# A masked and a cross attention block with a two-expert mixture on one core: another start-up, the second batch prepared three stages earlier, and the first and last self-attention prepared by halves

## The chip, the core and the metric

The kernel runs on one core of a Trainium2 chip. The core has five engines that run side by side, each with its own queue of instructions: TensorE (PE: matmuls and transposes), VectorE (DVE), ScalarE (ACT), GpSimd (POOL) and SyncE (SP, which here only starts DMAs). They meet through semaphores: an instruction that waits holds up everything behind it on its own engine. The metric is the time of one execution in microseconds (us), shorter being better.

## What is computed

Eight batches of 512 tokens of 256 numbers, 16 heads of 16. Per batch:

```python
x = x + tanh(g_xattn) * cross_attention(layernorm(x), ctx, ctx)      # no mask, no projections
n = layernorm(x)
h = n + self_attention(rmsnorm(n) * g1)       # q, k, v, o projections, rotary q and k, causal
y = h + mixture(rmsnorm(h) * g2)              # 8 experts, the best 2 of each token, 704 wide
out = x + tanh(g_ffn) * y
```

## The kernel before, in words

The program has two parts. The first (to about 1163 us) runs both attentions of all batches and scatters the routed tokens into `rows_in`; the second runs 71 tiles of 128 rows through the experts. The change touches the first part only.

**Units and stages.** An attention of one batch is four groups of four heads (g0 to g3). A group is done in two passes of 16 units. In a *max* unit PE multiplies a q tile with all k (L489, plus a mask matmul L492 for self-attention) and DVE takes the row maximum (`neg`, L811). In a *key* unit PE computes the transposed scores with the maximum folded in (L506, L509), ACT takes the exponential (`probs`, L680), and four value matmuls (L527) follow per key tile. Between the passes POOL splits the 16 maxima into three bfloat16 parts (`split_neg`, L1101 to L1104), PE turns them (`neg_turn`, L540), and ACT copies them and starts a DMA into the last rows of `q_stack` (L779, L781). q and k are used as three bfloat16 parts each (`parts_q`, `parts_k`), which are stored to DRAM (L384, six DMAs for each) and loaded back, six DMAs a group, as `q_stack[g]` and `k_stack[g]` (L377). There is one pair of these buffers for each group number.

**Steps.** `Step(i)` is a turn of eight stages s = 0..7, each of 16 places u. In step i the batch `cross` = i+1 is in cross attention, `own` = i in self-attention, `past` = i-1 finishes its self-attention and its output, and `ahead` = i+2 is prepared. Every engine walks the same steps, i from -2 to 8, and at fixed places u its `extra` function does the side work. `max_of(s)` and `main_of(s)` say which group has its max pass and which its key pass in a stage: stages 0 to 3 have the max passes of `cross`, 4 to 7 those of `own`; the key passes run two stages behind. A stage that has both passes is called double here, one with a single pass single. Below, c0 g2 is group 2 of the cross attention of batch 0, o7 that of the self-attention of batch 7.

**Side work.** For `ahead`: DVE statistics of x (stage 3), POOL normalises (`xq`), PE turns x and ctx (stages 4 and 5, `aux`), ACT copies to `flat_q`, `flat_k`, POOL splits into parts, SP stores them. For the next `own`, in stage 7: DVE adds the cross attention into x1 and takes statistics, POOL normalises (`xn`), and at the start of the next step ACT makes `hn1`. PE turns `hn1` at u = 4, 8; it projects q at 12, 13, 16, 17, k at 20, 21, 24, 25 and v at 31, 32, 37, 38, all through the one PSUM bank `aux`, which ACT empties after each half of 128 columns. DVE and POOL rotate q and k, POOL (in step 7 DVE for q) splits them. For `past`: output projection `wo` (u = 58 to 63), `h`, its root mean square (ACT squares, POOL `r_h`, L1082), router, and `scatter` (eight indirect DMAs on POOL, L1180). In every step -1 to 6 POOL also splits the weights of one expert in eight *pieces* (`split_piece`, L1074 to L1078), pieces 0 to 5 in stages 0 to 5, 6 and 7 in stage 6. A piece waits until the store of the piece before has landed, since both use the one buffer `w_parts`:

```python
step.wait(pool, m["w_in_ld"], (e * n + (k + 1)) * 16)
step.wait(pool, m["w_part_st"], (e * n + k) * 16)
```

Step -2 has no attention: it prepares batch 0 through `aux` alone. Step 7 (`LAST`) has the key passes o6 g2, g3 in stages 0, 1, no attention in 2 and 3, the max passes of o7 in 4 to 7 and key passes o7 g0, g1 in 6, 7; step 8 has o7 g2, g3.

## Time and profile before

| | us |
|---|---|
| three timed runs, median (lowest to highest) | 1715.73 (1715.44 to 1720.02) |
| profiled execution, its own time | 1707.33 |
| its span, first to last instruction | 1705.6 |
| PE, DVE, POOL, ACT busy, of the span | 1482.6, 976.2, 932.4, 807.1 |
| mean granted clock of PE | 0.946 of 2.4 GHz |

The profiled execution lies 8.4 us below the median of the timed runs. PE being busy for 87% of the span does not mean that it is at its peak all that time: in many stages its matmuls wait for their partners, and busy intervals include that pipelining. Places in the program are found by time: the first max matmul starts at 40.96, step 1 begins at 246.9, step 7 at 1010.6, the last exponential ends at 1114.4, the second part begins at about 1164.

### The profile page before, as it was taken

How to read it: one execution, taken by the hardware profiler on the slowest of the kernel's cores; microseconds unless marked ns; L12 is line 12 of the kernel's file. 1: busy time of each engine (PE TensorE's matmuls, PEld its weight loads, DVE VectorE, ACT ScalarE, POOL GpSimd, SP SyncE). 2: the span in 40 equal slices, each digit the busy share in tenths (PEclk: the TensorE clock that was granted, in tenths of full speed). 3: DMA queues.
4: the chain of work that ended last, by engine and by line, in shares of the span. 5: the costliest groups of instructions: out<-in, count | busy, mean ns of one | idle time of the engine just before them, and what ended most of it. 6: DMA issues, size and time to landing. Idle time of an engine off the chain costs nothing. (4 is left out here: it accounts for less than half of the span.)

```text
span 1705.6 us, 33019 instructions
## 1 busy us (share of the span) xinstructions
PE 1482.6 (87%) x9936; PEld 936.1 (55%) x9936; DVE 976.2 (57%) x2345; ACT 807.1 (47%) x1845; POOL 932.4 (55%) x1153
## 2 busy tenths in 40 slices
PE   1966989999999989989989987942999999999997
PEld 0212344444444444444443443432999999999997
DVE  1826667677677677677677555522444444444443
ACT  0451755755755755755755753521333333333332
POOL 5276766678678678678678353221334334433443
PEclk9987999989989999999999988966999999999999
DMA  5545564556455555556455434116142443244211
GB/s 171 156 128 157 162 180 134 155 158 199 151 171 186 155 173 183 160 173 186 147 182 163 145 121 111 63 37 255 54 147 60 151 150 122 93 151 151 61 57 32
DMA packets 112509, 238.41 MB, mean 140 GB/s; under 512 B 20624, under 2 KB 74772, under 8 KB 110295
## 3 DMA queue, kind: packets, MB, share of 16 engines
q1 hardware_dynamic: 76198, 147.66, 28.4%
q0 software_dynamic: 22656, 78.48, 13.4%
q10 hardware_dynamic: 13488, 10.17, 2.2%
q8 instruction: 91, 1.49, 0.4%
q14 instruction: 76, 0.61, 0.1%
HBM read 144.14 MB, written 93.14 MB: 139 GB/s over the span
## 5 line engine op out<-in xcount | busy, mean ns | idle before, releaser
L811 DVE TENSOR_REDUCE neg<-max_ps 128x1 f32<-128x512 f32 (+3 forms) x1024 | 564.6, 585 | 297.9 <-PE max_ps L492 150.1
L680 ACT ACTIVATE probs<-key_ps 128x512 f32<-128x512 f32 (+3 forms) x1024 | 499.5, 520 | 348.8 <-PE key_ps L509 197.8
L489 PE MATMUL max_ps<-k_stack,q_stack 96*128 96x512 bf16 (+3 forms) x1024 | 365.4, 362 | 75.0 <-DVE neg L811 33.9
L506 PE MATMUL key_ps<-q_stack,k_stack 99*128 99x512 bf16 (+3 forms) x1024 | 356.1, 351 | 22.7 <-ACT probs L680 17.5
L489 PEld LDWEIGHTS max_ps<-k_stack,q_stack 96*128 96x128 bf16 x1024 | 102.2, 100 | 293.3 <-DVE neg L811 173.4
L506 PEld LDWEIGHTS key_ps<-q_stack,k_stack 99*128 99x128 bf16 x1024 | 101.6, 100 | 153.4 <-ACT probs L680 92.7
L1448 PE MATMUL y_ps<-weights,hidden_t 128*128 x1278 | 171.4, 290 | 4.8 <-issue 3.4
L1448 PEld LDWEIGHTS y_ps<-weights,hidden_t 128*128 128x128 f32 x1278 | 158.3, 194 | 6.7 <-issue 6.7
L1424 PE MATMUL gate_ps<-weights,rows_t 128*128 x852 | 156.2, 332 | 6.5 <-DMA weights<-w_split 5.3
L1348 DVE TENSOR_TENSOR hidden<-silu,up_ps 128x352 f32<-128x352 f32 x142 | 74.0, 521 | 137.4 <-PE up_ps L1424 137.4
L1424 PE MATMUL up_ps<-weights,rows_t 128*128 x852 | 148.4, 323 | 0.0
L1295 POOL TENSOR_TENSOR more<-part,so_far 128x256 f32<-128x256 f32 x71 | 51.9, 731 | 175.3 <-issue 120.2
L527 PE MATMUL pv_ps<-probs,v_cross 128*32 128x512 f32 x1024 | 137.7, 605 | 4.5 <-ACT out_t L774 4.5
L1424 PEld LDWEIGHTS gate_ps<-weights,rows_t 128*128 128x128 f32 x852 | 137.1, 190 | 8.1 <-issue 7.9
L1424 PEld LDWEIGHTS up_ps<-weights,rows_t 128*128 128x128 f32 x852 | 139.0, 189 | 0.0
L1395 ACT ACTIVATE hidden_t<-hid_ps 128x512 fp32r<-128x512 f32 (+1 forms) x142 | 61.9, 488 | 151.7 <-PE hid_ps L1437 151.7
L1285 POOL DMA_INDIRECT so_far<-out,whose x71 | 73.0, 1028 | 101.8 <-issue 52.1
L1374 ACT ACTIVATE rows_t<-rows_ps,g_sb 128x128 fp32r<-128x128 f32 x142 | 44.4, 364 | 163.7 <-PE rows_ps L1409 163.7
L492 PE MATMUL max_ps<-squares_b 128*128 128x128 bf16 x512 | 117.7, 230 | 0.0
L509 PE MATMUL key_ps<-squares_b 128*128 128x128 bf16 x512 | 115.4, 226 | 0.0
L1299 POOL DMA_INDIRECT out<-more,whose x71 | 72.7, 1024 | 60.6 <-POOL more L1295 57.1
L527 PE MATMUL pv_ps<-probs,v_own 128*32 128x512 f32 (+3 forms) x1024 | 104.0, 477 | 1.7 <-ACT out_t L774 0.7
(182 smaller groups left out, 2115.8 us busy)
## 6 DMA issues: line engine op xcount, KB each, us to landing
w_split<-w_parts POOLq DMA_DIRECT2D x32, 704.0 KB
weights<-w_split SPq DMA_DIRECT2D x8, 2816.0 KB, 11.0
weights<-w_split SPq DMA_DIRECT2D x8, 1280.0 KB, 13.1
rows<-rows_in ACTq DMA_DIRECT2D x71, 129.0 KB
w_split<-w_parts POOLq DMA_DIRECT2D x16, 512.0 KB
kept_sb<-kept SPq DMA_DIRECT2D x16, 512.0 KB, 5.8
parts_cross_q<-parts_q SPq DMA_DIRECT2D x48, 128.0 KB
parts_cross_k<-parts_k SPq DMA_DIRECT2D x48, 128.0 KB
```

The source lines that it names most:

```text
L489: r = mm(ps[:, 0:keys], q_stack[g][0:KROWS, hd, qt * P:(qt + 1) * P], k_stack[g][0:KROWS, hd, 0:keys], start=True, stop=not own)
L492: r = mm(ps[:, qt * P:keys], ident_b, mask_qk, start=False, stop=True)
L506: r = mm(ps[:, q0:S], k_stack[g][0:KROWS + NEGROWS, hd, kt * P:(kt + 1) * P], q_stack[g][0:KROWS + NEGROWS, hd, q0:S], start=True, stop=no ...
L509: r = mm(ps[:, q0:q0 + P], ident_b, mask_kq, start=False, stop=True)
L527: mm(pv_ps[32 * hd:32 * hd + 32, q0:S], v_of["own" if own else "cross"][:, kt, g * HG + hd, :], probs[:, kt % 2, hd, q0:S], start=(kt == 0 ...
L680: act.activation(probs[:, kt % 2, hd, q0:S], key_ps[j % 2][:, q0:S], ACT.Exp).then_inc(m["exp_done"], 1)
L811: v.tensor_reduce(neg[:, g % 2, hd, qt:qt + 1], max_ps[(n * 16 + j) % MAX_RING][:, 0:keys], op=ALU.max, axis=AX.X, negate=True).then_inc(m ...
L1285: g_.indirect_dma_start(out=so_far[j % 2][:, :], out_offset=None, in_=out_rows, in_offset=bass.IndirectOffsetOnAxis(ap=whose[j % OWNERS][: ...
L1299: g_.indirect_dma_start(out=out_rows, out_offset=bass.IndirectOffsetOnAxis(ap=whose[j % OWNERS][:, 0:1], axis=0), in_=more[j % 2][:, :], i ...
L1348: v.tensor_tensor(hidden[:, n * FH:(n + 1) * FH], silu[:, n * FH:(n + 1) * FH], up_ps[n][:, 0:FH], ALU.mult)\
L1424: r = mm(ps[n][:, 0:FH], rows_t[:, a, c, :], weights[:, bass.ds(off + (w_ * WALL + at + c * F + n * FH), FH)], start=(c == 0 and (a, w_) = ...
L1448: r = mm(y_ps[:, 0:D], hidden_t[:, a, k, :], weights[:, bass.ds(off + (w_ * WALL + 2 * WG + k * D), D)], start=(k == 0 and (a, w_) == PASS ...
```

## The change

- **Start-up.** Step -2 is gone. Batch 0 is prepared by code of its own: the `k_stack` memsets go from POOL to DVE; SP loads the identity second and most constants late; PE turns ctx first and then x into four free banks; k half 0, q half 0 and q half 1 are split by DVE, k half 1 by POOL. SP then issues the loads of x and ctx of batch 1 (the latter waits for POOL's copy `v_cross`), stores half 0 of k and q, loads group 0, and stores half 1. Halves have their own semaphores.
- **Steps -1 and 0.** x and ctx of batch 1 are prepared in stages 0 to 2 of step -1 (statistics in stage 0, turned at u = 24, 28, 32, 36). The max passes of c1 are in stages 4 to 7 of step -1, its key passes in stages 0 to 3 of step 0. Step 0 has no max pass in stages 0 to 3 and no key pass in 4 and 5. Nothing changes in stages 6 and 7 of step 0.
- **Steps 0 and 7 (`alone`).** `hn1` is turned at u = 2, 4; the projections come as q0, k0, q1, k1, each whole at one place (6, 8, 10, 12), in step 0 v at 14 and 17. DVE rotates and splits each q half as it comes, POOL each k half in stage 0. SP stores q0, k0, loads group 0, then stores q1, k1.
- **Pieces.** Expert e is now split in step e, not e-1: none in step -1; in step 7 two in each of the stages 4 to 7. In step 7 both scatters of batch 5 come after the k split, in stage 1.
- The seven stores of `padding` move from the start to step 0. In steps 1 to 6 each engine does the same work in the same order.

```diff
     def max_of(self, s):
-        u = self.named("cross" if s < 4 else "own")
+        if self.i == -1 and s >= 4:
+            return ("cross", 1, 1, s - 4)
+        u = None if self.i == 0 and s < 4 else self.named("cross" if s < 4 else "own")
         return u and (*u, s % 4)
 
     def main_of(self, s):
-        which, g = [("past", 2), ("past", 3), ("cross", 0), ("cross", 1), ("cross", 2), ("cross", 3), ("own", 0), ("own", 1)][s]
-        u = self.named(which)
+        order = FIRST_MAINS if self.i == 0 else MAINS
+        which, g = order[s]
+        u = which and self.named(which)
         return u and (*u, g)
 
     def tail_of(self, s):
-        return self.main_of(s - 1) if s else self._past(1)
+        return self.main_of(s - 1) if s else Step(self.i - 1).main_of(7)
 
     def neg_of(self, s):
-        return self.max_of(s - 1) if s else self._past(3)
-
-    def _past(self, g):
-        u = self.named("past")
-        return u and (*u, g)
+        return self.max_of(s - 1) if s else Step(self.i - 1).max_of(7)
+
+
+MAINS = [("past", 2), ("past", 3), ("cross", 0), ("cross", 1), ("cross", 2), ("cross", 3), ("own", 0), ("own", 1)]
+FIRST_MAINS = [("cross", 0), ("cross", 1), ("cross", 2), ("cross", 3), (None, 0), (None, 0), ("own", 0), ("own", 1)]
...
 PIECES_AT = ((0,), (1,), (2,), (3,), (4,), (5,), (6, 7), ())
-
-
-def splits_on_dve(step):
-
-    return step.i in (-2, LAST)
+LAST_PIECES_AT = ((), (), (), (), (0, 1), (2, 3), (4, 5), (6, 7))
+
+
+def alone(step):
+
+    return step.i in (0, LAST)
+
+
+def turned_at(step):
+
+    return (24, 28, 32, 36) if step.i == -1 else (72, 76, 80, 84)
+
+
+def parts_made(step, b, c, n, of_own):
+
+    if of_own and alone(step) or not of_own and b == 0:
+        return b * 6 + 3 * c + n + 1
+    return b * 6 + 2 * (n + 1)
...
+def qk_order(step):
+
+    return [("q", 0), ("k", 0), ("q", 1), ("k", 1)] if alone(step) else [("q", 0), ("q", 1), ("k", 0), ("k", 1)]
...
+                    if step.i == 0:
+                        for n in range(SPARE):
+                            sp.dma_start(rows_in[E * CAP + n * P:E * CAP + (n + 1) * P, :], padding[:, :]).then_inc(m["ld_pad"], 16)
...
-                sp.wait_ge(m["ready_v"], 1)
-                for n in range(SPARE):
-                    sp.dma_start(rows_in[E * CAP + n * P:E * CAP + (n + 1) * P, :], padding[:, :]).then_inc(m["ld_w"], 16)
-                def sp_body(step):
-                    if step.i == -2:
-
-                        store_parts(step, "cross", "q", 0, "x_parts", "x_st")
-                        store_parts(step, "cross", "k", 0, "c_parts", "c_st")
-                        load_stack(step, "cross", 0, 0, 0)
...
+                sp.dma_start(rope_sb[:, :, :], c_rope).then_inc(m["ld_const"], 16)
+                sp.dma_start(g1_sb[:, :], g1.rearrange("(c p) -> p c", p=P), allow_slow_non_contiguous=True).then_inc(m["ld_const"], 16)
+                sp.dma_start(g2_sb[:, :], g2.rearrange("(c p) -> p c", p=P), allow_slow_non_contiguous=True).then_inc(m["ld_const"], 16)
+                load_x(Step(-1))
+                first = Step(-2)
+                store_half(first, "k", "c", 0, 0)
+                store_half(first, "q", "x", 0, 0)
+                load_stack(first, "cross", 0, 0, 0)
+                store_half(first, "k", "c", 0, 1)
+                store_half(first, "q", "x", 0, 1)
+
+                run_steps(sp, body)
...
-                        for c, at in enumerate((4, 8)):
+                        for c, at in enumerate((2, 4) if alone(step) else (4, 8)):
                             if u == at:
                                 step.wait(pe, m["x1_norm"], own + 1)
                                 turn("hn1", own, c, hn1)
-                        for k, at in enumerate((12, 13, 16, 17)):
+                        halves = qk_order(step)
+                        for k, at in enumerate((6, 6, 8, 8, 10, 10, 12, 12) if alone(step) else (12, 13, 16, 17, 20, 21, 24, 25)):
...
+                    if own is not None and alone(step):
+                        for c, where_ in enumerate(((0, 2, 0), (0, 3, 2))):
+                            if at == where_:
+                                own_half(step, c)
...
...
+                dve.wait_ge(m["x_ld"], 16)
+                for t in range(QT):
+                    r = v.bn_stats(st_x[:, t, :], x_in[:, t, :])
+                chain.link(r)
+                for t in range(QT):
+                    r = v.bn_aggr(mv_x[:, t, :], st_x[:, t, :])
+                r.then_inc(m["x_stat"], 1)
+                aux_free(dve, "c", 0, 0)
+                split(flat_k, parts["k"], 0, "c_parts", 0)
+                for c in range(DC):
+                    aux_free(dve, "x", 0, c)
+                    split(flat_q, parts["q"], c, "x_parts", 3 * c)
...
                     for s in range(8):
-                        if s == 0 and step.cross is not None:
-                            load_piece(step.cross, 0)
-                        if s == 0 and done is not None:
+                        if s == 0 and step.own is not None:
+                            load_piece(step.own, 0)
+                        if s == 0 and done is not None and step.i != LAST:
                             scatter(done, 0)
                         extra(step, s)
-                        if s == 1:
+                        if s == 1 and not alone(step):
                             rotate(step, 1)
+                        if s == 2 and step.i == -1:
+                            split_ahead(step, "k")
                         ng = step.neg_of(s + 1) if s < 7 else Step(step.i + 1).neg_of(0)
-                        pieces_ = PIECES_AT[s] if step.cross is not None else ()
+                        pieces_ = (LAST_PIECES_AT if step.i == LAST else PIECES_AT)[s] if step.own is not None else ()
                         for k in pieces_[:-1]:
                             split_piece(step, k)
                         if ng and s:
                             split_neg(step, ng)
-                        if s == 1:
+                        if s == 1 and step.i == -1:
+                            split_ahead(step, "q")
+                        if s == 1 and not alone(step) or s == 0 and alone(step):
                             rotate(step, 2)
+                        if s == 1 and done is not None and step.i == LAST:
+                            scatter(done, 0)
+                            scatter(done, 1)
                         for k in pieces_[-1:]:
                             split_piece(step, k)
-                        if s == 0 and done is not None:
+                        if s == 0 and done is not None and step.i != LAST:
                             scatter(done, 1)
                         if ng and not s:
                             split_neg(step, ng)
 
...
+                split(None, flat_k, parts["k"], "c_parts", 0, 1)
+                g_.tensor_scalar(v_of["cross"][:, :, :, 0:DH].rearrange("p t h d -> p (t h) d"),
+                                 ctx_in[:, :, :].rearrange("p t (h d) -> p (t h) d", d=DH), 1.0, 0.0, ALU.mult, ALU.add)\
+                    .then_inc(m["v_cross"], 1)
```

SP at the start of the program; `parts_cross_k` and `parts_cross_q` are the stores of batch 0, `q_stack` and `k_stack` the loads of its groups. Before:

```order
L439 DMA rows_in<-padding 128x258 x7
L384 DMA parts_cross_q<-parts_q 8x16x512 x6
L384 DMA parts_cross_k<-parts_k 8x16x512 x6
L377 DMA q_stack<-parts_cross_q 48x1x2048
L377 DMA q_stack<-parts_cross_q 32x1x2048
```

After:

```order
L383 DMA x_in<-in_x 128x4x256
L387 DMA ctx_in<-in_ctx 128x4x256
L412 DMA parts_cross_k<-parts_k 8x16x512 x3
L412 DMA parts_cross_q<-parts_q 8x16x512 x3
L407 DMA q_stack<-parts_cross_q 48x1x2048
```

Group 0 is loaded after six stores in place of twelve, and the input loads of batch 1 now stand ahead of the first store.

PE in stage 0 of step 7, from the turn of the first half of `hn1` (the key matmuls of o6 g2 between). Before, to the first projections of q:

```order
L559 MATMUL aux<-ident,hn 128x128 x4
L506 MATMUL key_ps<-q_stack,k_stack 128x256
L509 MATMUL key_ps<-squares_b 128x128
L506 MATMUL key_ps<-q_stack,k_stack 128x256
L509 MATMUL key_ps<-squares_b 128x128
L527 MATMUL pv_ps<-probs,v_own 32x384 x4
L506 MATMUL key_ps<-q_stack,k_stack 128x256
L509 MATMUL key_ps<-squares_b 128x128
L506 MATMUL key_ps<-q_stack,k_stack 128x256
L509 MATMUL key_ps<-squares_b 128x128
L552 MATMUL turn_ps<-ident,out_t 128x128 x4
L566 MATMUL aux<-hn_t,sb_wq 128x512
```

After, from the first projection of q to that of the second half:

```order
L620 MATMUL aux<-hn_t,sb_wq 128x512 x2
L560 MATMUL key_ps<-q_stack,k_stack 128x384
L563 MATMUL key_ps<-squares_b 128x128
L560 MATMUL key_ps<-q_stack,k_stack 128x384
L563 MATMUL key_ps<-squares_b 128x128
L594 MATMUL turn_ps<-squares_b,neg_parts 48x128
L620 MATMUL aux<-hn_t,sb_wk 128x512 x2
L560 MATMUL key_ps<-q_stack,k_stack 128x256
L563 MATMUL key_ps<-squares_b 128x128
L560 MATMUL key_ps<-q_stack,k_stack 128x256
L563 MATMUL key_ps<-squares_b 128x128
L581 MATMUL pv_ps<-probs,v_own 32x384 x4
```

A projected half now stands every two key units, where before one stood every four.

POOL in step 7, from the root mean square of `h` (batch 6) on; `neg_parts` is the split of the maxima of o7 g0, then g1. Before:

```order
L1081 TENSOR_SCALAR tmp_r<-ss 128x4
L1082 TENSOR_TENSOR r_h<-tmp_r,half 128x4
L1101 TENSOR_SCALAR neg_parts<-neg 128x16
L1102 TENSOR_TENSOR neg_rest<-neg,neg_parts 128x16
L1103 TENSOR_SCALAR neg_parts<-neg_rest 128x16
L1104 TENSOR_TENSOR neg_parts<-neg_rest,neg_parts 128x16
```

After, from the end of g0's split to the start of g1's:

```order
L1207 TENSOR_TENSOR neg_parts<-neg_rest,neg_parts 128x16
L1177 TENSOR_SCALAR w_parts<-w_in 128x704
L1178 TENSOR_TENSOR w_parts<-w_in,w_parts 128x704
L1166 DMA w_in<-in_L_ffn_wu 128x704
L1181 DMA w_split<-w_parts 256x1x704
L1177 TENSOR_SCALAR w_parts<-w_in 128x704
L1178 TENSOR_TENSOR w_parts<-w_in,w_parts 128x704
L1166 DMA w_in<-in_L_ffn_wu 128x704
L1181 DMA w_split<-w_parts 256x1x704
L1204 TENSOR_SCALAR neg_parts<-neg 128x16
```

Piece 0 stands before g0's split, pieces 1 and 2 between g0 and g1, 3 and 4 between g1 and g2, 5 and 6 between g2 and g3.

## Rows read from the trace of the kernel before

**Rows 1.** Timeline of the start: start us, us, engine line op out<-in xcount [idle before]
```profile
10.95 1.33 DVE L875 BATCH_NORM_STATS2 st_x<-x_in 128x6 f32<-128x256 f32 x4
...
14.63 2.17 POOL L1091 TENSOR_SCALAR xq<-x_in,less_mean,r_x 128x256 f32<-128x256 f32 x4
...
25.83 6.42 SPq L384 DMA_DIRECT2D parts_cross_k<-parts_k  x6
...
28.91 2.12 POOL L1056 TENSOR_TENSOR parts_k<-rest,parts_k 128x1024 bf16<-128x1024 f32 x1
31.12 1.05 POOL L1157 TENSOR_SCALAR v_cross<-ctx_in 128x1024 f32<-128x1024 f32 x1
...
34.54 1.91 SPq L377 DMA_DIRECT2D q_stack<-parts_cross_q  x3
...
40.96 13.93 PE L489 MATMUL max_ps<-k_stack,q_stack 96*128 96x512 bf16 x24 [17.26 <-DMA k_stack<-parts_cross_k]
```
**Rows 2.** Groups by line, DVE: names, shapes, count | busy, mean ns | idle before
```profile
L1338 DVE MEMSET weights<- 64x1024 f32 x1 | 0.9, 912 | 8.8 <-PEq L238 8.8
```
**Rows 3.** Timeline between c0 and c1, the same columns
```profile
126.72 2.00 PE L489 MATMUL max_ps<-k_stack,q_stack 96*128 96x512 bf16 x4 [12.70 <-DMA k_stack<-parts_cross_k]
...
140.59 1.12 PE L559 MATMUL aux<-ident,hn 128*128 128x128 f32 x4 [11.86 <-ACT hn L700]
```
**Rows 4.** Busy time in stretches: stretch length, PE PEld DVE ACT POOL, clock, DMA
```profile
40.96:51.20 10.24, 10.16 (x18) 1.81 (x18) 9.62 (x17) 0.00 (x0) 0.00 (x0) 1.00 1.01 297
...
74.20:87.90 13.70, 13.11 (x74) 3.95 (x76) 12.07 (x27) 9.84 (x21) 7.25 (x14) 1.00 0.24 81
...
99.80:111.60 11.80, 10.75 (x62) 2.99 (x61) 0.68 (x2) 10.03 (x19) 11.06 (x9) 1.00 0.40 134
...
1010.60:1022.40 11.80, 10.03 (x78) 4.65 (x71) 1.25 (x4) 9.04 (x24) 7.15 (x12) 1.00 0.41 148
1022.40:1036.20 13.80, 13.76 (x87) 6.14 (x86) 11.10 (x20) 8.49 (x21) 1.92 (x2) 1.00 0.25 78
1056.90:1063.90 7.00, 6.36 (x35) 2.81 (x32) 6.85 (x17) 0.00 (x0) 0.00 (x0) 0.61 1.01 193
...
1105.40:1114.40 9.00, 8.02 (x72) 3.04 (x70) 0.68 (x2) 6.71 (x17) 3.86 (x4) 1.00 0.17 61
```
**Rows 5.** Timeline of step 7: a projected half, the end of `wo`, the first max matmul
```profile
1018.89 1.10 PE L566 MATMUL aux<-hn_t,sb_wq 128*128 128x512 f32 x2
...
1021.35 0.59 ACT L686 ACTIVATE flat_q<-aux 128x512 f32<-128x512 f32 x1
...
1046.86 1.99 PE L575 MATMUL aux<-sb_wo,own_t 128*128 128x256 f32 x8 [0.88 <-DVE h L891]
...
1056.52 0.29 PE L489 MATMUL max_ps<-k_stack,q_stack 96*128 96x128 bf16 x1 [7.67 <-DMA k_stack<-parts_own_k]
```
**Rows 6.** Timeline of POOL: pieces, their stores and the waits before them
```profile
123.86 0.40 POOL L1074 TENSOR_SCALAR w_parts<-w_in 128x256 fp32r<-128x256 f32 x1 [2.98 <-DMA w_split<-w_parts]
...
182.96 0.74 POOL L1078 DMA_DIRECT2D w_split<-w_parts  x1
...
189.25 0.78 POOL L1074 TENSOR_SCALAR w_parts<-w_in 128x704 fp32r<-128x704 f32 x1 [4.41 <-DMA w_split<-w_parts]
...
192.69 0.72 POOL L1078 DMA_DIRECT2D w_split<-w_parts  x1
...
198.38 0.78 POOL L1074 TENSOR_SCALAR w_parts<-w_in 128x704 fp32r<-128x704 f32 x1
```
**Rows 7.** Timeline of POOL in steps 7 and 8
```profile
1052.18 1.04 POOL L1082 TENSOR_TENSOR r_h<-tmp_r,half 128x4 f32<-128x4 f32 x1
...
1130.05 0.20 POOL L1081 TENSOR_SCALAR tmp_r<-ss 128x4 f32<-128x4 f32 x1 [19.67 <-ACT sq L733]
```
**Rows 8.** Timeline of ACT in step 8: the DMA of g3's maxima, the last exponential
```profile
1101.07 0.73 ACTq L781 DMA_DIRECT2D q_stack<-neg_rows  x1
...
1113.90 0.45 ACT L680 ACTIVATE probs<-key_ps 128x128 f32<-128x128 f32 x2 [0.51 <-PE key_ps L509]
```

346 lines of the change are left out of this document (213 added, 133 removed).

## The prediction, as written before the changed kernel ran

> **What bounds the kernel now.** I read the page for what is busy, the timeline for the three stretches that the change touches, the busy time by stage for prices, and the waits of POOL. In the middle of the program the stages are full: a double stage takes 13.7 us with PE busy for 13.1 [rows 4], and steps 1 to 6 are not changed. The time that could be won lies at both ends. At the start PE first has a max matmul at 40.96, held by the stack loads [rows 1]. Between the first and the second cross attention PE waits 12.7 us for loads and then 11.9 us for `hn1` [rows 3]. In step 7 PE has finished `wo` at 1048.85 and waits 7.67 us for the stacks of o7 [rows 5]. POOL is nowhere the bound as a whole, but it is one queue, and the maxima of each group pass through it.
>
> All times below stand against the profiled execution (span 1705.6); I carry the difference over to the median.
>
> **Start-up: 9.0 us less.** The four memsets cost DVE 2048 elements each; at the 912 ns for 1024 elements of [rows 2] that is 1.82 us each, 7.3 in all, from 0.75 to 8.05, and the small ones to 8.4. The statistics then begin 2.55 us before the 10.95 of [rows 1], and `xq` ends at 14.3 in place of 16.8. POOL splits k half 1 (half of 1.05 + 2.12 twice, with gaps 3.5) and copies `v_cross` (1.05): 19.0. Only then may SP issue ctx of batch 1 (0.55), and only behind it the stores: six at 0.61 (last three rows of six stores each take that) end at 23.3. From the last store's issue (32.25) to the first load's (34.54) is 2.3 us, and from there to the first matmul 6.4 [rows 1]: 25.6 and 32.0. DVE has q half 0 ready at 18.5, so it hides. 40.96 - 32.0 = 9.0. A bfloat16 memset on DVE isn't in the trace: at half the time all of this would come 3.6 us sooner, at half as much again 3.6 later; I take the float row, as the nearest.
>
> The Trainium skill ("VectorE: DVE Perf Modes", Zero memsets can be issued as uint32) says that a memset takes one cycle per element whatever the type, which agrees with taking the float row and speaks against the quicker case. The Trainium skill ("SBUF — State Buffer", Who interferes with whom) also says that a DVE instruction with two SBUF inputs and a GpSimd instruction that reads SBUF exclude each other; no row of before shows the two side by side in the start. By that rule DVE's two subtracts of a half (some 0.6 us each) could push `v_cross`, and the gain would be about 8 in place of 9.
>
> **From the first max pass to step 1: 4.0 us more.** Before it is 246.9 - 41.0 = 205.9, with both waits of [rows 3] in it. Prices: a single cross max stage 9.65 (10.2 to the next, DVE-bound), a double stage 13.7, a single cross key stage 11.8 with two turns of `aux`, so 11.5 without [rows 4]. After, step -1: stage 0 is 9.65 + 2.1 for the statistics that move into it = 11.8; stage 1 10.1 with two turns; stages 2 to 5 double, 13.8 + 13.5 + 13.6 + 13.6; stage 6 9.65 + 0.7 for the last cross group; stage 7 9.65 + 5.0 for x1's sums and statistics on DVE, which nothing hides now = 14.7. Together 101.5. POOL has no pieces there, so `xn` is ready when the stage ends. The stack loads of c1 are ready by my count some 3 us before each is due: the k split ends at about 68, the stores land at 72, g0 is loaded by 78 and due at 81.
>
> Step 0, stage 0, is the price of packing. A whole projected half is two calls of 1.10 on PE [rows 5]; behind it on PE stands the next key matmul (0.35), on ACT its exponential (0.6) and then the copy out of `aux` (0.59) before the next half may start: 4.0 us each, and only two key units go by. So: `hn1` 2.0 from the stage's start, two turns with copies 5.0, four halves 16.0, v, its copy and the last units 4.4: 27.4. In stage 1 the rest of v: 13.8. Stages 2, 3: 11.5 each. Stages 4, 5, single max passes of o0: 7.0 each as [rows 4] shows for o7, 7.2 + 7.8 with turns. But POOL must in these 15 us split q (6.7), g0's maxima, piece 4 (3.6), k (6.7) and g1's maxima: 4.2 us late in stage 5, 0.5 in stage 6. Stages 6 and 7 as before, 12.4 + 12.1. Together 108.4. 101.5 + 108.4 = 209.9, against 205.9. The idle 24.6 us go, but what was a double stage becomes single ones (six doubles in place of eight), and stage 0 grows. Bounds: if the halves fit between key units as they do before, 8 us less, that is 4 us better than before; if POOL is later by one piece's landing, 5 more.
>
> **Step 7 up to the max passes of o7: 1.1 us less, not 7.7.** Before, stages 0 and 1 took 11.8 + 13.8 = 25.6, all projections and half of v in them; stage 1 of step 8, with a group and nothing beside it, is 9.0 [rows 4]. After, stage 0 by the same handover (4.0, less 0.2 for shorter exponentials): 2.0 + 4.5 + 15.2 + 1.2 = 22.9, stage 1 9.3: 32.2, 6.6 more. `wo` ends at 1048.85 + 6.6 = 1055.4. The stacks have long landed then: the k parts of half 0 are ready at about 1032.5, and 2.3 + 6.4 later is 1041.8. So the DMA wait of 7.67 goes, and PE's own order takes its place; 1055.4 against 1056.5.
>
> **The pieces in step 7: 16.8 us more.** (Times here are in before's clock; the parts above shift them all.) `r_h` ends at 1053.2 [rows 7]; it follows `h`, which follows `wo`, so it comes 6.6 later, 1059.8. Everything behind it on POOL is one chain: a piece, then the landing of its store, since the next piece waits for that. A 704-wide piece takes 193.41 - 189.25 = 4.16. From the end of a store's issue to the next piece are 189.25 - 183.70 = 5.55, and another piece did not have to wait after 4.97 [rows 6]. I take 5.0 for pieces 0 to 3, since little else moves in step 7. For a 512-wide store POOL copied `v_cross` (1.1) and then waited 2.98 [rows 6]: 4.1. Pieces of 512 and 256 take 3.6 and 2.8, scaled from the same rows. Up to g3's split: four pieces 16.6, four landings 20.0 (the base of `out`, 3.6, lies in the last), then 3.6, 4.1, 3.6, 4.1, 2.8 and the split 1.1: 55.9. So g3's maxima are split at 1115.7. From there it is 1.0 to ACT's DMA, and from that to the end of the exponentials 1114.35 - 1101.07 = 13.3 [rows 8]: 1130.0. Before it is 1114.35: 15.7 later, and as this holds the 1.1 won above, the pieces cost 16.8. PE waits for each split at its place, so the stalls show at the turns of g1 (some 6), g2 (5) and g3 (4); behind a turn on PE are the second half of the stage's units, and ACT and DVE wait for those. After piece 7 POOL scatters batch 6 (13 us), done at about 1133; what it owes next is `r_h` of batch 7, which started at 1130.05 [rows 7] and now would near 1146: hidden. The second part starts later by the same 15.7.
>
> **Sum.** -9.0 + 4.0 - 1.1 + 16.8 = +10.7 us: a span of 1716.3, and 1715.7 + 10.7 = 1726.4 for the timed median.
>
> **Rivals.** (1) *The middle wins more than I count.* The halves of step 0 fit between key units and POOL keeps up in stages 4 and 5: -9.0 - 4.0 + 15.7 = +2.7, 1718.4. For it: 24.6 us of idle time do go [rows 3]. Against: `aux` is one bank, and four handovers stand in eight places. (2) *The pieces in step 7 are covered*, the one that ends faster. Six landings stand in the chain, 28.2 us. If they averaged 2.9 instead of 4.7 the whole change would come to zero, and from 1.9 down no turn waits: -9.0 + 4.0 - 1.1 = -6.1, 1709.6. For it: step 7 moves little else. Against: the shortest landing in the rows is 4.1. A better start and middle with half the stalls gives about the same time. (3) *More stalls.* Landings 0.6 longer each, as in [rows 6], make 3.6; and the clock granted after PE's idle 7.67 us was 0.61 [rows 4], which behind three stalls may add 4: 1734. (4) *The start doesn't come sooner*, since the first store still stands behind POOL's copy: with that at 25 in place of 19, 6 of the 9 us are lost: 1732.
>
> **How the numbers follow.** Changes under 0.3% (5 us) can't be told from none here. Forecast, 3 to 17 us slower: 0.55, of which 0.03 under 5 us. Rival 1: 0.19, within. Rival 2 and what leads to its time: 0.16. Rival 3: 0.06, rival 4: 0.04. Slower: 0.52 + 0.10 = 0.62; within 0.22; faster 0.16. The range leaves out rival 2's lower half and what lies beyond rival 3: 1710 to 1734.
>
> **What would show it.** First max matmul at 32; start of step 1 at 242; the first max matmul of o7 right behind `wo` with no DMA wait, in absolute time 6 us earlier (9 - 4 + 1); gaps of PE before the turns of g1, g2 and g3 in steps 7 and 8, ended by POOL's splits, with POOL waiting for `w_split`; last exponential at about 1125. I am wrong if those turns don't wait, or if stage 0 of steps 0 and 7 takes under 20 us.

## The result and the profile after

The changed kernel takes 1733.55 us (median of six, 1729.14 to 1738.29), the kernel before 1718.44 (1715.44 to 1721.94): a ratio of 1.0087, 95% interval 1.0064 to 1.0110, or 11 to 19 us slower. Forecast was 10.7 slower and 1726.4, in a range of 1710 to 1734: the result lies 0.5 us inside its upper end, and the kernel before itself came out at 1718.44 here, where the forecast had been added to 1715.73.

The span can be cut at six events that every trace shows: the first max matmul, the first reduction of c2 (start of step 1), the first exponential of o6 g2 (start of step 7), the first reduction of o7, the last exponential, the end. Each entry below is the difference of two start or end times of such rows. Both kernels were profiled twice.

```
kernel           to first   to      steps   step 7 up  passes  to the  span
                 max mm     step 1  1 to 6  to o7      of o7   end
before             41.0     206.0   763.6     46.4      57.4    591.2   1705.6
before, again      41.0     205.7   766.1     46.0      58.7    590.1   1707.6
changed            36.4     210.2   769.6     45.3      77.3    592.7   1731.4
changed, again     36.4     210.1   765.9     45.5      74.6    591.7   1724.3
forecast change    -9.0      +4.0     0       -1.1     +16.8     0       +10.7
measured (means)   -4.6      +4.3    +2.9     -0.8     +17.9    +1.6     +21.3
```

The profiles differ by 21 us where the timed medians differ by 15. Both profiles of before lie below its median (1707.3 and 1709.4 of a median of 1714 to 1720 in the later comparisons), so single profiles are good for the place of a change, not for its last microseconds.

The start after (timeline: start us, us, engine, line, operation, out<-in, count), which answers to [rows 1]:

```profile
18.58 0.98 DVE L910 TENSOR_TENSOR turned<-flat_q,parts_q 128x512 f32<-128x512 f32 x1
...
19.59 1.26 DVE L911 CAST parts_q<-turned 128x512 bf16<-128x512 f32 x1
...
20.66 1.10 POOL L1346 TENSOR_SCALAR v_cross<-ctx_in 128x1024 f32<-128x1024 f32 x1
20.89 1.40 DVE L913 TENSOR_TENSOR parts_q<-turned,parts_q 128x512 bf16<-128x512 f32 x1
21.84 0.37 SPq L387 DMA_DIRECT2D ctx_in<-in_ctx  x1
22.25 2.02 SPq L412 DMA_DIRECT2D parts_cross_k<-parts_k  x3
...
24.32 1.81 SPq L412 DMA_DIRECT2D parts_cross_q<-parts_q  x3
...
29.81 1.90 SPq L407 DMA_DIRECT2D q_stack<-parts_cross_q  x3
...
36.37 1.98 PE L543 MATMUL max_ps<-k_stack,q_stack 96*128 96x512 bf16 x4 [17.62 <-DMA k_stack<-parts_cross_k]
```

Two things are to be seen: the first store is issued right behind POOL's copy and the ctx load, at 22.25, and DVE's split of q half 0 ends only at 22.29.

POOL in step 7 after (timeline), which answers to [rows 6] and [rows 7]: `r_h`, the pieces, g3's split.

```profile
1066.16 1.05 POOL L1185 TENSOR_TENSOR r_h<-tmp_r,half 128x4 f32<-128x4 f32 x1
1067.21 0.77 POOL L1177 TENSOR_SCALAR w_parts<-w_in 128x704 fp32r<-128x704 f32 x1
...
1083.86 0.78 POOL L1177 TENSOR_SCALAR w_parts<-w_in 128x704 fp32r<-128x704 f32 x1 [4.22 <-DMA w_split<-w_parts]
...
1097.57 2.34 POOL L1271 TENSOR_TENSOR base_sb<-base_sb,kept_sb 128x1024 f32<-128x1024 f32 x1
...
1117.39 0.40 POOL L1177 TENSOR_SCALAR w_parts<-w_in 128x256 fp32r<-128x256 f32 x1 [4.27 <-DMA w_split<-w_parts]
...
1121.10 0.22 POOL L1207 TENSOR_TENSOR neg_parts<-neg_rest,neg_parts 128x16 bf16<-128x16 f32 x1
```

And the stages there (busy time in stretches: length, then PE PEld DVE ACT POOL, granted clock, DMA share, GB/s), from stage 0 of step 7 to the last exponential; before, the first three are 11.8, 13.8 and 20.7 long [rows 4, 5]:

```profile
1016.10:1036.90 20.80, 17.25 (x92) 7.58 (x85) 10.08 (x19) 10.76 (x27) 4.71 (x8) 0.92 0.26 89
1036.90:1046.70 9.80, 8.88 (x72) 3.94 (x71) 7.25 (x11) 6.83 (x17) 6.86 (x7) 1.00 0.28 73
1046.70:1061.40 14.70, 10.41 (x53) 7.48 (x51) 1.93 (x4) 2.88 (x5) 8.15 (x11) 0.88 0.82 223
1061.40:1069.70 8.30, 5.65 (x30) 1.76 (x30) 6.84 (x18) 3.75 (x12) 7.14 (x8) 0.88 0.58 170
1069.70:1078.80 9.10, 8.03 (x41) 4.82 (x41) 6.36 (x17) 1.68 (x4) 5.27 (x10) 0.55 0.34 122
1078.80:1097.60 18.80, 17.21 (x119) 9.24 (x119) 11.09 (x37) 7.33 (x19) 10.65 (x16) 0.64 0.41 138
1097.60:1115.20 17.60, 12.96 (x100) 6.46 (x101) 12.31 (x30) 7.30 (x18) 9.79 (x13) 0.81 0.59 206
```

The key stages of o7 g0 and g1 take 18.8 and 17.6 where they took 12.6 and 12.3 before, and 13.4 and 13.7 in its second profile (first exponential of a group to that of the next). PE looks busy in the first of them, at a granted clock of 0.64, near the lower of its two levels (1.2 of 2.4 GHz); the matmuls stretch to fill the time that POOL's chain leaves.

The largest waits of PE in the passes of o7 (timeline): the turns of the maxima of g0, g1 and g3 wait for POOL, the third unit of g3's max pass for DVE. The turn of g2, at 1109.20, does not wait.

```profile
1072.65 0.30 PE L594 MATMUL turn_ps<-squares_b,neg_parts 128*48 128x128 bf16 x1 [0.89 <-POOL neg_parts L1207]
...
1089.20 0.30 PE L594 MATMUL turn_ps<-squares_b,neg_parts 128*48 128x128 bf16 x1 [1.46 <-POOL neg_parts L1207]
...
1103.10 0.29 PE L543 MATMUL max_ps<-k_stack,q_stack 96*128 96x128 bf16 x1 [3.87 <-DVE neg L883]
...
1121.38 0.24 PE L594 MATMUL turn_ps<-squares_b,neg_parts 128*48 128x128 bf16 x1 [1.67 <-POOL neg_parts L1207]
```

### The profile page after: what moved, and what is told of

It is laid out like the page before. It is cut to its first block and busy times, and to the rows that moved or that the text cites. A ratio compares the mean times of both kernels' runs of the same rounds, so it can differ in the third digit from the quotient of the medians.

```text
span 1731.4 us, 33153 instructions
## 1 busy us (share of the span) xinstructions
PE 1505.1 (87%) x9936; PEld 943.1 (54%) x9936; DVE 1007.8 (58%) x2375; ACT 806.3 (47%) x1845; POOL 914.4 (53%) x1155
## 3 DMA queue, kind: packets, MB, share of 16 engines
q0 software_dynamic: 22656, 78.48, 13.3%
## 5 line engine op out<-in xcount | busy, mean ns | idle before, releaser
L1535 ACT ACTIVATE hidden_t<-hid_ps 128x512 fp32r<-128x512 f32 (+1 forms) x142 | 61.9, 488 | 151.6 <-PE hid_ps L1577 133.8
L1425 POOL DMA_INDIRECT so_far<-out,whose x71 | 73.0, 1028 | 101.5 <-issue 44.3
```

Of the source, the lines that this page charges most:

```text
L1425: g_.indirect_dma_start(out=so_far[j % 2][:, :], out_offset=None, in_=out_rows, in_offset=bass.IndirectOffsetOnAxis(ap=whose[j % OWNERS][: ...
```

## The experiments

Both kernels were profiled once more, and ten further kernels ran; each was timed beside the kernel before on the same chip. One table for the ten, in the cuts of the first, from one profile each; the ratio is that of timed runs to the kernel before.

```
run            first  to      steps   to o7  passes  end    ratio (95%)
               mm     step 1  1 to 6         of o7
pieces_early   37.9   216.8   769.5   45.3   57.9   591.1   1.0047 (1.0026 to 1.0068)
ctx_later      31.3   211.0   766.0   45.3   73.0   589.9   1.0039 (1.0015 to 1.0063)
mid_before     39.6   212.7   765.9   45.4   62.1   591.0   0.9997 (0.9979 to 1.0014)
spread         36.4   210.7   773.6   44.7   77.0   596.2   1.0086 (1.0061 to 1.0111)
two_parts      36.0   206.3   770.8   47.3   67.2   590.4   1.0004 (0.9986 to 1.0022)
before_swap    40.8   206.6   768.6   47.5   60.2   587.7   0.9980 (0.9956 to 1.0004)
last_early     36.4   207.3   768.7   45.5   73.7   592.0   1.0063 (1.0034 to 1.0093)
all_three      31.3   205.6   765.6   47.3   67.8   595.9   1.0000 (0.9968 to 1.0033)
all_swap       31.4   203.2   759.0   45.3   69.8   592.8   0.9959 (0.9935 to 0.9983)
final          31.2   203.3   759.2   45.3   62.9   593.8   0.9905 (0.9869 to 0.9941)
```

### Both kernels again

Each was profiled once more, unchanged.

> The kernel before, unchanged, profiled a second time. In its first profile steps 1 to 6 (from the first max group of c2 to the second exponential group of step 7's stage 0) take 763.6 us, and in the profile of the changed kernel 769.6, though their work and order are the same. If that is a price of the change, this run shows 763 to 765 again and a span near 1706. If it is only the spread of one execution (the timed runs of before reach 1721.9, 14 above its profile), this run shows a middle of 766 to 770 and a span of 1711 to 1718.

> The changed kernel, unchanged, profiled a second time. First max reduction at 37, step 1 at 246 to 247, steps 1 to 6 in 765 to 770, last exponential of own attention 7 some 122 to 123 after step 7's start (before: 103.8). If the half clock at 1070 to 1100 belongs to the order of step 7 it is there again; if it came by chance it is gone, and the last exponential comes 5 or more sooner.

Steps 1 to 6 of before came at 766.1, those of the changed kernel at 765.9. So the 6 us of the first pair were mostly spread, yet not all (below). The passes of o7 took 74.6, at a clock of 0.75, so the low clock belongs to the order of step 7. The turns of g0, g1 and g3 waited 2.4, 2.5 and 1.5, that of g2 not at all, as in the first profile.

### The pieces one step sooner (pieces_early)

```diff
-LAST_PIECES_AT = ((), (), (), (), (0, 1), (2, 3), (4, 5), (6, 7))
+FIRST_PIECES_AT = ((), (), (0,), (1,), (2,), (3,), (4, 5), (6, 7))
...
-                    e = step.own
+                    e = step.cross
...
```

> As the changed kernel, but each weight piece is split one step sooner: step -1 takes expert 0's (stages 2 to 7), and step 7 has none. My theory (the pieces of step 7 cost 16.8 by my count, 19.9 by the traces): the max and key passes of o7 take 50 to 58 us from the first reduction to the last exponential in place of 77, and the whole is 15 to 20 us shorter than the changed kernel: 1714 to 1719, some 0.2% below before to equal; step -1 grows by 0 to 4 us. Rival (the time went to the low clock that PE's idle stages in step 7 bring, not to the pieces): the granted clock in the max passes of o7 stays at 0.6, the passes still take 65 us or more, and the whole is 1725 or more.

The o7 passes, first reduction to last exponential (busy time in a stretch):

```profile
1069.50:1127.40 57.90, 51.64 (x429) 25.18 (x430) 33.77 (x102) 32.67 (x86) 19.09 (x33) 0.94 0.21 69
```

57.9, as before the change: the 18 us there are the pieces. The clock is 0.94 over the stretch, so the rival falls. But the total won only 7 us against the changed kernel's ratio of 1.0087. In steps -1 and 0 the pieces cost 6.7 and at the start 1.5: c1's first group waited 3.3 us for its `k_stack`, `hn1` came 2.7 us later. I had put 0 to 4 on that. There was nothing to spare for it: in the changed kernel itself c1's first stacks landed at 83.5 and PE waited 0.5 us for them, where the prediction had counted on 3 us in hand.

### The context load behind the first stacks (ctx_later)

```diff
-                load_x(Step(-1))
                 first = Step(-2)
+                first.wait(sp, m["x_norm"], 1)
+                sp.dma_start(x_in[:, :, :], x_d[1]).then_inc(m["x_ld"], 16)
...
                 store_half(first, "q", "x", 0, 1)
+                aux_full(sp, "c", 0, DC - 1)
+                first.wait(sp, m["v_cross"], 1)
+                sp.dma_start(ctx_in[:, :, :], ctx_d[1]).then_inc(m["ctx_ld"], 16)
```

> As the changed kernel, but the load of batch 1's context, which waits for POOL's copy of v_cross, is issued behind the first eighteen stores and loads instead of ahead of them. My theory (the first store waits for that copy, which ended at 21.8): the first store is issued at about 19.5 when the first half of q is split, the first max matmul comes at 33.5 to 34.5 instead of 36.4, and the whole is 2 to 3 us shorter. Rival (POOL's own split of k's second half ends late too, or the loads' landing sets the time): under 1 us.

```profile
16.65 2.02 SPq L412 DMA_DIRECT2D parts_cross_k<-parts_k  x3
...
18.71 4.18 SPq L412 DMA_DIRECT2D parts_cross_q<-parts_q  x3
...
24.94 1.90 SPq L407 DMA_DIRECT2D q_stack<-parts_cross_q  x3
...
31.34 1.98 PE L547 MATMUL max_ps<-k_stack,q_stack 96*128 96x512 bf16 x4 [12.60 <-DMA k_stack<-parts_cross_k]
```

The first max matmul came 5.0 us sooner, twice what I expected. The stores ended 3.2 us sooner, at 22.9, now waiting for q's last part (DVE, 22.3) and not for POOL's copy; and the time from the last store to the first load was 2.1 in place of 3.7. What else is in that 1.6 was not taken apart; the load of ctx, issued just ahead of the stores in the changed kernel, no longer runs beside them. Of these 5 us 0.8 is lost on the way to step 1 (211.0 against 210.2). The ratio fell by more than 2 to 3 us (from 1.0087 to 1.0039, some 8 us), of which the start explains 5.

### The start and step 7 alone (mid_before)

Taken back: max passes of c1 in step 0, batch 1 prepared in stages 4 to 6 of step -1, step 0 as before, pieces a step sooner.

```diff
-        if self.i == -1 and s >= 4:
-            return ("cross", 1, 1, s - 4)
-        u = None if self.i == 0 and s < 4 else self.named("cross" if s < 4 else "own")
+        u = self.named("cross" if s < 4 else "own")
...
-    return (24, 28, 32, 36) if step.i == -1 else (72, 76, 80, 84)
+    return (72, 76, 80, 84)
```

> Only the new start-up and the halves of step 7: batch 1 is prepared in step -1's stages 4 to 6 and c1's max passes stand in step 0's stages 0 to 3, as before, step 0 projects as before, and the pieces stand where they did before. My theory (the parts add up): first max matmul at 36.4 to 37.9, from it to step 1 205.9 as before, step 7 up to the max passes of o7 45.4 (before 46.2), the passes of o7 58: 4 to 5 us shorter than before. Rival (the idle in step 0 ends with a load that comes no sooner, so the early start is given back there): step 1 still starts at 246 to 247, the interval from the first matmul grows to 209 or more, and the whole is 0 to 1.5 us shorter than before.

The rival holds in what it says of the gain, though step 1 began later than it said, at 252.2. The start itself is worth only 1.4 us when the first weight piece is loaded, split and stored beside it (the first stacks landed 3.2 us later than in the changed kernel). The two waits of [rows 3] came back, 12.4 and 12.1 us, and from the first matmul to step 1 it took 212.7 in place of 206. Of that, 5.5 us are one wait:

```profile
PE max_ps L529 <- DMA k_stack<-parts_cross_k: 5.5, 1, 5.5
```

It stands at 251.6: the seven stores of `padding`, which the change put into step 0, are issued from 227.0 to 230.4 ahead of the stores of c2's parts, and group 0 of c2 landed at 251.5, in the second profile of before at 246.2. In the changed kernel step 0's stacks are ready sooner and the same stores delay nobody. Without that wait step 1 would begin near 246.7 (an estimate: 252.2 less 5.5), where it begins in before: with the old middle the sooner start is given back, and the stores of `padding` in step 0 make it worse. The passes of o7, with no piece in them, took 62.1 and not the 58 expected; with the 57.4 to 60.2 of the other profiles without pieces there, that is how far this stretch moves when nothing of the pieces is in it.

### Halves further apart (spread)

```diff
-                        for k, at in enumerate((6, 6, 8, 8, 10, 10, 12, 12) if alone(step) else (12, 13, 16, 17, 20, 21, 24, 25)):
+                        for k, at in enumerate((6, 7, 10, 11, 14, 15, 18, 19) if alone(step) else (12, 13, 16, 17, 20, 21, 24, 25)):
...
-                        for t, at in enumerate((14, 14, 17, 17) if step.i == 0 else (31, 32, 37, 38)):
+                        for t, at in enumerate((22, 23, 26, 27) if step.i == 0 else (31, 32, 37, 38)):
...
```

> As the changed kernel, but in steps 0 and 7 the halves of q and k are projected at every fourth unit (6, 10, 14, 18) instead of every second (6, 8, 10, 12), v of step 0 at 22 and 26. My theory (each half waits for the copy of the half before it, behind a key unit: 4 us for a half whose neighbours are two units off): stage 0 of step 0, 26.0 now, and stage 1, 13.3, together lose 6 to 8; stages 0 and 1 of step 7, 20.6 + 9.8, lose 3.5 to 5, if the stacks of o7 still land before wo ends; the whole 8 to 12 us shorter than the changed kernel. Rival (PE's work and the arrival of hn1 set those stages, not the handovers): both change by under 2 us, or the stacks become the last and o7's first max matmul waits for a load as before.

My theory fell. Stages 0 and 1 of step 0 took 21.8 + 16.1 in place of 25.8 + 13.3, 1.2 less in all, and what was won there was gone by the end of step 0; up to o7 step 7 won 0.7. The packing moves time between two stages, it does not cost 4 us a half. It also tells of the pieces: the o7 passes took the same 77.0 us, but with PE busy for 55.2 of them in place of 61.5 and at a clock of 0.84 in place of 0.78. With the faster matmuls the waits show: the turns of g0, g1 and g3 waited 4.6, 4.8 and 1.5, in place of 0.9, 1.5 and 1.7. Not PE and not its clock set this stretch.

### Two buffers for the pieces (two_parts)

```diff
-s1("w_parts", 2, F, dt=F32R)
+s1("w_parts", 2, 2, F, dt=F32R)
...
-                    step.wait(pool, m["w_part_st"], (e * n + k) * 16)
+                    half_ = k % 2
+                    step.wait(pool, m[f"w_part_st{half_}"], (e * n // 2 + k // 2) * 16)
...
```

> As the changed kernel, but two buffers take the split weight pieces in turn, so that a piece waits for the store of the piece before the last. My theory (in step 7 POOL's chain of pieces and landings sets the turns of g1 to g3; seven landings of 4 us lie in it): the maxima of g3 are split some 12 to 20 us sooner, no turn of step 7 waits, and from the first reduction of o7 to the last exponential it takes 58 to 65 in place of 75 to 77; whole 12 to 18 shorter than the changed kernel. Rival (the half clock of the stretch, which lies in order and idle of PE, sets it): 70 or more, and under 5 us on the whole.

```profile
1060.30:1127.50 67.20, 55.01 (x430) 26.11 (x430) 37.80 (x102) 33.13 (x86) 44.46 (x63) 0.89 0.43 146
```

67.2: half way, between the 58 to 65 expected and the 70 of the rival. Without most of the landings 8.8 of the 17.9 us go. The rest goes with POOL's own work there (44.5 us busy in 67, 15.0 of 57.4 in before) and what it does to DVE, shown below; how it divides was not measured. A second gain I had not expected lies in step 0, 3.9 us: the interval to step 1 fell to 206.3, since stage 4 of step 0 takes 9.2 when POOL's pieces there don't wait, in place of 12.7:

```profile
195.10:204.30 9.20, 7.87 (x57) 4.21 (x56) 7.19 (x18) 3.11 (x6) 4.29 (x5) 1.00 0.86 268
```

### The maxima ahead of the second scatter (before_swap)

```diff
+                        if ng and not s:
+                            split_neg(step, ng)
                         if s == 0 and done is not None:
                             scatter(done, 1)
-                        if ng and not s:
-                            split_neg(step, ng)
```

> The kernel before with one exchange: in stage 0 of each step POOL splits the maxima of c's first group ahead of the second scatter of the past batch, not behind it. Reason: in the profiles stage 1 of steps 2 to 6 takes 17.7 in some steps and 18.5 to 23 in others; where it is long, POOL stood for the landing of the first scatter, its split of the maxima ended 7 to 8 us after the reductions, PE's turn waited 1.4 to 1.6 for it, and the granted clock then fell to 0.6. My theory: that turn no longer waits in any step, stage 1 takes 17.5 to 17.9 in all of them, steps 2 to 6 take 630 or less (631 and 634 before; 637 to 641 in the changed kernel), and the whole is 1 to 5 us shorter than before and its spread smaller. Rival (the clock falls there for PE's own sparse stage, and q's rotation comes later instead): no change, or up to 3 us longer.

Inconclusive in time (0.9980, up to 1.0004). Stage 1 took 17.8 in four of the five steps 2 to 6 and 21.5 in one, where the turn did not wait at all. So my reason was wrong. Nor did steps 2 to 6 get shorter: they took 638.3, against 631.2 and 634.2 in before and 630 or less expected, since stage 0 took 15.7 to 16.0 in each step where it took 15.0 in both profiles of before. Then I looked at what DVE did in the long stages 1. In the second profile of the changed kernel, step 4:

```profile
657.02 2.13 POOL L1156 TENSOR_TENSOR rest<-flat_q,parts_q 128x1024 f32<-128x1024 f32 x1
...
657.12 2.58 DVE L917 TENSOR_TENSOR with_cos<-flat_k,rope_sb 128x512 f32<-128x512 f32 x1
...
660.97 0.39 PE L543 MATMUL max_ps<-k_stack,q_stack 96*128 96x512 bf16 x1 [2.26 <-DVE neg L883]
```

and at the same place of step 4 in the later run all_swap:

```profile
641.77 0.72 DVE L921 TENSOR_TENSOR with_cos<-flat_k,rope_sb 128x512 f32<-128x512 f32 x1
642.04 2.44 POOL L1160 TENSOR_TENSOR rest<-flat_q,parts_q 128x1024 f32<-128x1024 f32 x1
...
643.79 0.39 PE L547 MATMUL max_ps<-k_stack,q_stack 96*128 96x512 bf16 x1 [0.42 <-DVE neg L887]
```

DVE's multiply of two SBUF operands takes 0.7 us when it comes first, and 2.58 when POOL's subtract started 0.1 us ahead of it: 0.55 us and the 2.03 that POOL still had to go. So it is in the fourteen traces, five such stages each, wherever the subtract had a lead of 0.1 us or more: the multiply takes 0.55 us and what POOL still has to go. Once the lead was 0.015 us, and it was the subtract that took longer (2.68). In 26 of the 70 the multiply took under 1 us, and stage 1 took 18.0 on the mean; in 33 it took 1.5 us or more, and the stage took 19.9 (18.6 to 23.1). The two go together; no run changed the multiply alone. In three of the 33, one each in both profiles of before and in before_swap (the 21.5), the subtract had not begun, and the 1.57 us began beside the cast that POOL makes ahead of it. In the long stage shown above PE idles 2.3 us for DVE, and in the 4.6 us that follow the granted clock is 0.63:

```profile
657.00:661.00 4.00, 1.74 (x20) 0.91 (x19) 4.00 (x6) 1.01 (x4) 3.67 (x3) 1.00 0.22 66
661.00:665.60 4.60, 4.60 (x16) 3.06 (x17) 4.23 (x10) 0.55 (x2) 2.08 (x2) 0.63 0.10 29
```

The Trainium skill ("SBUF — State Buffer", Who interferes with whom) says that a DVE instruction with two SBUF inputs contends with a GpSimd instruction that reads SBUF, the later one being blocked as a whole; these rows agree, in both directions, but for some 0.14 us: the multiply was 1.9 longer, where POOL had 2.03 to go, and the subtract 0.31 longer, where DVE had 0.45 to go.

### Five pieces ahead of o7 (last_early)

```diff
-LAST_PIECES_AT = ((), (), (), (), (0, 1), (2, 3), (4, 5), (6, 7))
+LAST_PIECES_AT = ((0, 1, 2), (3, 4), (), (), (), (5,), (6,), (7,))
...
+                        if step.i == LAST and s < 2:
+                            for k in pieces_:
+                                split_piece(step, k)
+                                if s == 1:
+                                    scatter(done, k - 3)
...
```

> As the changed kernel, but five of step 7's eight weight pieces are split before the max passes of o7: 0 to 2 in stage 0 ahead of k's halves, 3 and 4 in stage 1 beside the scatters; 5, 6 and 7 follow the maxima in stages 5 to 7. Nothing is left out, one buffer as before. My theory (what costs is the place: eight pieces and their landings between the r_h of batch 6 and g3's maxima): three pieces are left there, the passes of o7 take 58 to 62 in place of 75 to 77, and the whole is 13 to 18 us shorter than the changed kernel. Rival (POOL's time in step 7 is short everywhere): k's second half is split later, so the stacks of o7 land behind wo, the first max matmul of o7 waits 3 us or more, and half of the gain is lost.

73.7: nearer to the rival. Its cause came true in part. Behind pieces 0 to 2 the split of k's second half ended 3.4 us ahead of o7's first max matmul, where it ended 10.3 ahead in the changed kernel; g0's stacks were still in time, but g1's `k_stack` came 5.5 us late. Pieces 3 and 4 beside the scatters kept POOL from g0's maxima, whose turn waited 5.4 us. No later turn waited: the waits moved from the turns of g1 and g3 to the beginning, and nearly the whole gain was lost.

### Combinations (all_three, all_swap, final)

all_three is ctx_later, two_parts and last_early together; all_swap adds the exchange of before_swap.

> The changed kernel with three edits together: the context load of batch 1 behind the first stacks, two buffers for the split pieces, and five pieces of step 7 ahead of o7. If the prices of the single runs add up: first max matmul at 31.3, from it to step 1 206 to 207, step 7 up to the passes 45 to 47, the passes of o7 57 to 61: step 1 starts at 238, and the whole is 8 to 14 us shorter than before (ratio 0.992 to 0.995). Rival (they share one gain, the buffers mattering only where the pieces stand late, or steps 2 to 6 give it back, which took 637 to 641 in four profiles with the new middle and 631 and 634 in two of before): ratio 0.997 or more.

> The same with the exchange that was made alone in before_swap: in stage 0 POOL splits the maxima of c's first group ahead of the second scatter. In before_swap stage 1 took 17.8 in four of the five steps 2 to 6, and here it takes 18.5 to 20 without the exchange. My theory: stage 1 takes 17.8 in most steps and steps 2 to 6 take 632 to 635 in place of 637 to 641, so the whole is 3 to 6 us shorter than the run without the exchange. Rival: one step in five loses 4 us all the same to the low clock, and no difference shows.

all_three matched before (1.0000): start and middle came as added up (31.3 and 205.6), but two pieces and the scatters stood ahead of g0's maxima again, and the passes of o7 took 67.8, not 57 to 61. With the exchange the multiply came ahead of POOL's subtract in all five steps, stage 1 took 18.0 in each, and steps 1 to 6 took 759.0 in place of 765.6. It helps not by the wait I had named; that POOL's time in stage 1 then no longer hangs on the landing of a scatter is my reading of the order, which no run separates. The two instructions pass each other by 0.3 us, so this is a matter of luck in another kernel.

final has pieces 0 and 1 ahead of k's halves, one behind each of g0, g1, g2, and three behind g3:

```diff
-LAST_PIECES_AT = ((), (), (), (), (0, 1), (2, 3), (4, 5), (6, 7))
+LAST_PIECES_AT = ((0, 1), (), (), (), (2,), (3,), (4,), (5, 6, 7))
...
```

> The changed kernel with the context load behind the first stacks, two buffers for the split pieces, the exchange of stage 0, and the pieces of step 7 put where POOL stood idle: 0 and 1 in stage 0 ahead of k's halves, 2, 3 and 4 each behind the maxima of g0, g1 and g2, 5 to 7 behind those of g3; none between k's second half and g0's maxima. My theory (the turns of g1 to g3 waited for pieces ahead of the maxima, and in the two runs before this for two pieces ahead of g0's): no turn of step 7 waits 1 us or more, no load holds o7's max passes, these take 57 to 60 (before 57.4 to 60.2, the changed kernel 75 to 77), from the first matmul to step 1 203 to 206, steps 2 to 6 631 to 633: a span near 1690, a ratio of 0.987 to 0.991. Rival (the pieces behind g3's maxima push the scatter of batch 6 and the r_h of batch 7, so that the routing and the second part begin later): from the last exponential to the end 597 or more in place of 590 to 593, and a ratio of 0.993 or more.

```profile
1039.10:1102.00 62.90, 56.56 (x429) 26.90 (x430) 35.64 (x102) 32.88 (x86) 35.01 (x53) 0.84 0.39 126
```

1697.94 us, median of six, a ratio of 0.9905 (0.9869 to 0.9941) to the kernel before: it beats both kernels. No turn of o7's maxima waits more than 0.2 us, and the passes take 62.9; 57 to 60 was expected. PE is busy for 56.6 of them, where the same matmuls took 52.1 of the 57.4 before, at a clock of 0.92. The stretch to the end is 593.8, 2.6 and 3.7 more than in the two profiles of before, and short of the 597 of the rival.

## Why the prediction was right, and where not

That the change costs time, and that the pieces in step 7 make it so, was right and is shown. The total came near by errors of both signs; term by term:

**Start: -9.0 forecast, -4.6 measured.** The mechanism was right, the sizes of three terms were not. The statistics began at 9.78, not at 8.4: the memsets took 1.76 each (the float row was the right neighbour), but with 0.38 between them and from 1.23 on. POOL's split of k half 1 took 4.4 and not 3.5. And "DVE has q half 0 ready at 18.5" failed: it was ready at 22.3, 1.9 for the later `xq` and 1.8 because DVE and POOL split side by side and held each other up (1.26 for a cast that took 0.43 with the next half, 1.40 and 0.98 for subtracts that took 0.69). The rule was weighed at 1 us in all; it took 1.8 from DVE and 0.6 from POOL's split. Here POOL's copy ended at about the same time and hid it; in ctx_later it was what the stores waited for. The last 1.4 us are the 3.7 from the last store to the first load, for which I had taken before's 2.3. Rival 4 named the right instruction, POOL's copy ahead of the first store; it came at 21.8, half way between 19 and 25.

**First max pass to step 1: +4.0 forecast, +4.3 measured, by luck: its errors cancel.** Step -1 took 97.1 and not 101.5, for x1's sums and statistics fit into its last stage (11.9, forecast 14.7). Step 0 took 113.1 and not 108.4. Its stage 0 was near (25.8, forecast 27.4), though the reason given for it, the handovers, was refuted by spread. Stages 4 to 7 took 51.2 in place of 44.2: I priced a single max pass of o0 with the 7.0 of o7 [rows 4], and it takes 9.2 there even without a wait, and POOL, late by its pieces' landings, held `xq` for 2.0, a turn for 5.3 and another for 1.8. two_parts took 3.9 of this away.

**Steps 1 to 6: 0 forecast, +2.9 on the mean of two.** "Are not changed" holds for the order, not for the phase. Step 1 is 3.7 shorter on the mean (128.3 and 128.4 against 132.4 and 131.8), nearly all in its stage 0, where PE's wait for exponentials, 3.2 us at 251.6 in before, is 1.7; spread and last_early, whose step 1 is that of the changed kernel, took 131.5 and 133.8, so this is no firm gain. Steps 2 to 6 take 641.2 and 637.5 against 631.2 and 634.2, in two places. Stage 1 took 95.9 and 96.9 in the five steps, against 91.3 and 92.2, with DVE's multiply at 1.5 us or more in six of ten stages against three of ten. And stage 0 took 82.0 in the first profile of the changed kernel, against 75.2 in its second and in both of before. In nine of the fourteen profiles stage 0 takes 15.0 in each of these steps and in five 15.6 to 16.0 (one stage 18.8), and both lengths occur with and without the change. What sets either phase is open.

**Step 7 up to o7: -1.1 forecast, -1.1 and -0.6 measured.** PE's own order took the place of the wait for a load, as said; stages 0 and 1 took 30.6 (forecast 32.2).

**Pieces in step 7: +16.8 forecast, +17.9 measured (19.9 and 15.9 in the two pairs), and pieces_early shows that it is they.** The chain on POOL from `r_h` to g3's split took 54.1 (forecast 55.9), with 4.0, 4.2, 4.0, 3.6, 5.9 and 4.3 between the end of a store's issue and the next piece. The size is right for a chain with two errors in it: `r_h` came 2.2 later against the first matmul of o7 than forecast, behind the second scatter of batch 5, and from g3's split to the last exponential it took 17.4, not 14.3, at a clock of 0.90. The stalls did not show where they were forecast: at the turns of g1, g2 and g3 (6, 5, 4) they are 1.5, 0 and 1.7, in the second profile 2.5, 0 and 1.5, and that of g0, for which none was forecast, waits 0.9 and 2.4. The rest shows as matmuls stretched by the low clock and as one wait of 3.9 us (3.0 in the second profile) for DVE at g3's third unit. So the chain on POOL was right, and where PE would stand for it was not. DVE was held there by POOL: its routing work on a few elements took as long as the piece or base beside it,

```profile
1084.84 1.57 DVE L991 TENSOR_TENSOR gap<-top 128x4 f32<-128x4 f32 x1
...
1098.16 1.89 DVE L1020 TENSOR_TENSOR picked<-where,hot 128x32 f32<-128x32 f32 x2
```

both ending within 0.2 us of a POOL instruction with two inputs (1084.72 + 1.67, 1097.57 + 2.34). So the bottom line, 10.7 slower, is low against 15.1 (11 to 19). The profiles, which differ by 21.3, miss 10.6 against the forecast: the start 4.4, steps 1 to 6 2.9, the end 1.6, the pieces 1.1, the rest 0.6. The timed medians miss only 4.4, so these parts are not all in the usual execution.

**The rivals.** Rival 1 (the middle wins 4 more) needed the halves to fit and POOL to keep up in stages 4 and 5. two_parts lets POOL come nearer to that (the two turns still wait 3.4 and 2.3) and wins 3.9 of the 8 us, so the middle costs there what it cost before. Rival 2 (pieces covered) did not come, but its number, 1709.6, was beaten by final, which places the pieces where they are covered. Rival 3 was part of the truth in its clock, not in its landings.

## What to carry to other kernels

Filling an idle gap by pulling work forward pays only if the work that it displaces has a place: here the idle of 24.6 us was filled, and as step -1 no longer split pieces (three of its eight began near or in the idle time, at 115.9, 123.9 and 130.7 in before), every expert's pieces moved a step later and the last eight went into the one stretch where the critical engine waits for POOL after every group. Before moving a block of background work, list for each place what that engine owes next, and put the background behind it, never ahead. And where DVE and POOL both run two-input work, look for the long instance of an instruction that is otherwise short: here its excess was the other engine's remaining time, but for 0.14 us.

## What the runs showed of the hardware that was not expected

- A DVE instruction on 4 elements a partition can take 1.57 us, and a 0.7 us multiply 2.58, when a POOL `TENSOR_TENSOR` started just ahead of it; with 0.27 us of lead for DVE it is POOL that takes 0.3 longer (2.44 for 2.13).
- In stages 6 and 7 of step -1 DVE's reductions are the bound. From 112.3 PE stops for 0.2 to 0.35 us before most of its max matmuls; at 115.4 the granted clock falls to the lower level, 0.50 (1.2 GHz), and stays there through stage 7 and into step 0, until 142.7 (behind the fall PE also stops five times for 0.7 to 0.8 us):

```profile
110.00:121.60 11.60, 9.67 (x30) 2.76 (x27) 11.09 (x20) 0.98 (x3) 2.47 (x6) 0.73 0.27 69
121.60:133.50 11.90, 8.54 (x16) 1.68 (x16) 11.77 (x25) 1.12 (x4) 5.86 (x15) 0.50 0.01 3
133.50:159.30 25.80, 21.27 (x75) 8.43 (x75) 13.65 (x21) 13.04 (x28) 8.32 (x11) 0.82 0.36 116
```

In stage 7 it cost nothing, since DVE was the bound; what it cost in stage 0 of step 0, where PE is, was not separated.
